# A two-layer attention kernel: ScalarE's copies ahead of exponentials in a layer's first steps, and another order of the work at the image's end

## The chip, the cores and the metric

The kernel runs on one core of one Trainium2 chip. The core has five engines that run side by side and meet by semaphores: TensorE (PE; its weight loads are shown as PEld), VectorE (DVE), ScalarE (ACT), GpSimd (POOL) and SyncE (SP), which starts the DMAs. The metric is the device time of one execution in microseconds; the figure of a version is the median of its runs.

## The reference

Two self-attention layers over eight images of 64x64 pixels and 64 channels, in float32:

```
xf = x.reshape(b, 4096, 64)
f, g, hh = xf @ wf + bf, xf @ wg + bg, xf @ wh + bh         # 8, 8 and 64 wide
x = gamma0 * softmax(g @ f.T) @ hh + x                      # layer 0

q, k, v = x @ Wq + bq, x @ Wk + bk, x @ Wv + bv             # 64 wide each
attn = softmax(q @ k.T)                                     # rows i, columns j
x = gamma1 * attn.T @ v + x                                 # layer 1
```

Layer 1 multiplies by the transposed attention matrix, so a row's sum must be known before the row's exponentials are used: the row of `v` is scaled by the row's weights (`v_scaled`), and the unscaled exponentials are the moving operand.

## The kernel before, in words

An image is 4096 positions, in 32 blocks of 128. The program handles two images in one pass of a hardware loop (four passes), each engine with its own instruction stream. An image has three parts.

**Layer 0** (`chunk0`): four chunks of 1024 queries, 32 steps each: two score matmuls (L499), ScalarE's exponential (L809), value matmuls (L515), and beside them matmuls and maxima of a coming chunk (L471, L977).

**Layer 1** (`steps1`): 32 rows of 128 queries, each cut into four pieces of 1024 keys. One piece is one step; 128 steps, eight (u0 to u7, two rows) to a pass of `t`. A step is:
- TensorE: `scores1` (L607), eight matmuls into two of four banks. It waits for VectorE's result of two steps before, since the banks alternate;
- VectorE: L1145 reads the scores, scales them into `e_whole` and takes the minimum (`bias_ready`);
- ScalarE: L872, the exponential in place with its sum (`exp1_done`), and after a row's fourth piece L878, the weights of its pieces (`chunk_w`);
- VectorE: `weigh_chunks` (L1121 to L1125) and `weigh_values` (L1134) make the row's `v_scaled`;
- TensorE: `values1` (L619), seven steps behind the scores (LAG1 = 7), into the four `sum_banks`.

In the first eight steps of layer 1 `sum_banks` aren't yet in use for values, and other work goes through them, two pairs called pair_c and pair_d. In the order in which TensorE has it (`between_scores`): a projection of q and k; after u1 the second half of `v` (L439); after u2 and u3 the transposes of the image after next (L419, `turn_x`), copied by VectorE (L952); after u4, u5 and u6 its projections pj0 to pj3 (L429; pj1 and pj2 both after u5). ScalarE copies out `v` (`projected_v`, L825) and the projections (`projected0`, L820). Each pair is written again after its copy only: `turn_x(2)` waits for the copy of `v` (`v1_sb`), pj2 for the copy of pj0, pj3 for that of pj1, and the first `values1` for that of pj2 (`pj_act`).

**The turn**, at the image's end: the last `values1` run; in between TensorE transposes eight units of the stacked f and g of the image after next (`turn_stack`, L463) into the `score_banks`, each copied by ScalarE (`turned_unit`, L842, `unit_sb`); VectorE scans x for its largest magnitude (`scan_x`, two parts, L958); from it TensorE computes a bound by one small matmul (`bound_of_qk`, L454), and VectorE derives powers of two and scales q's and k's weights by them (`scales`, L964 to L972, `w1s_ready`); VectorE adds the residual (L1191, `o_dve`, four parts); TensorE turns the result back (`turn_back`, L629, parts 2, 3, 0, 1), and VectorE and ScalarE copy it out (L1197, L895).

Each engine runs its list strictly as written; the order is written out by hand, and the semaphore waits in it are all there is of a schedule.

Of the kernel before, what the change touches and what calls it, by code (L numbers as in the profile page):

```python
# [21 lines left out]
AX_X = mybir.AxisListType.X  # L22
# [8 lines left out]
def attention_pair_kernel(nc, x, wf, bf, wg, bg, wh, bh, gamma0, wq, bq, wk, bk, wv, bv, gamma1, out):  # L31
# [44 lines left out]
    UNITS = 2 * NCH  # L76
    SCANS = 2
# [8 lines left out]
    with ExitStack() as ctx:  # L86
# [7 lines left out]
        score_banks = ctx.enter_context(nc.psum_tensor("score_banks", [P, 4, BANK], F32))  # L94
# [25 lines left out]
        x_abs2 = sb("x_abs2", [P, SCANS], F32)  # L120
        x_abs = sb("x_abs", [P, 1], F32)
# [292 lines left out]
        def _(pe):  # L414
# [269 lines left out]
            def image_steps(image, par):  # L684
                for q in range(NCH):
                    chunk0(image, par, q)
                ahead, last = image + 2, NCH - 1
                pe.wait_ge(a_used, ((image + 1) * NCH + 1) * TILES + EARLY * ATN + FREE_A)
                pe.wait_ge(w1s_ready, image + 1)
                pe.wait_ge(mid_ready, image * NCH + 3 + FREE)  # L690
                project_qk(par, 0, pair_c)
                values0(image, par, last, T - 4)

                def first_scores():
                    pe.wait_ge(low_done, 2 * (image * NCH + 2))
                    pe.wait_ge(k_copied[0], 32 * (image + 1))
                    scores1(image, 0, 0, 0)

                pe.wait_ge(exp0_done, (image + 1) * NCH * T - 1 + FREE_ST)
                project_qk(par, 1, pair_a)  # L700
                for i in range(T - 3, T):
                    values0(image, par, last, i)
                last_sums0(image, last)
                project_qk(par, 2, pair_b)
                pick0(image, last)
                first_scores()
                spread0(image, last)
                project_v(0, pair_c)

                def between_scores(u):  # L710
                    if u == 0:
                        pe.wait_ge(mid_ready, image * NCH + 4 + FREE)
                        project_qk(par, 3, pair_d)
                    elif u == 1:
                        pe.wait_ge(v1_sb, 2 * image + 1)
                        project_v(1, pair_c)
                    elif u == 2:
                        pe.wait_ge(x_loaded, 16 * (ahead + 1))
                        pe.wait_ge(low_done, 2 * (image * NCH + 4))
                        turn_x(0, pair_d[:, 0, :])  # L720
                        turn_x(1, pair_d[:, 1, :])
                    elif u == 3:
                        pe.wait_ge(v1_sb, 2 * image + 2)
                        turn_x(2, pair_c[:, 0, :])
                        turn_x(3, pair_c[:, 1, :])
                    elif u == 4:
                        pe.wait_ge(xt_dve, ahead * RT + 2)
                        project0(par, 0, pair_d)
                    elif u == 5:
                        pe.wait_ge(xt_dve, ahead * RT + 4)  # L730
                        project0(par, 1, pair_c)
                        pe.wait_ge(pj_act, ahead * RT + 1)
                        project0(par, 2, pair_d)
                    elif u == 6:
                        pe.wait_ge(pj_act, ahead * RT + 2)
                        project0(par, 3, pair_c)

                def steps1(t, first):
                    for u in range(U1):
                        if first and u == 1:  # L740
                            pe.wait_ge(low_done, 2 * (image * NCH + 3))
                        if first and 0 < u < NCH:
                            pe.wait_ge(k_copied[u], 32 * (image + 1))
                        if not first or u > 0:
                            scores1(image, t * 2 + u // NCH, t * U1 + u, u)
                        if first:
                            between_scores(u)
                        if first and u == LAG1:
                            pe.wait_ge(pj_act, ahead * RT + 3)
                        if t == 1 and u == 1:  # L750
                            pe.wait_ge(pj_act, ahead * RT + 4)
                        if not first or u >= LAG1:
                            values1(image, t, u - LAG1)

                for t in range(T // 2):
                    steps1(t, t == 0)
                for u in range(U1 - LAG1, NCH):
                    values1(image, T // 2 - 1, u)
                pe.wait_ge(f_stacked, (ahead + 1) * 4)
                pe.wait_ge(g_stacked, (ahead + 1) * 4)  # L760
                for n in range(4):
                    pe.wait_ge(bias_ready, (image + 1) * STEPS1 - (1 if n < 2 else 0) + FREE_S1)
                    turn_stack(n, score_banks[:, n, :])
                pe.wait_ge(unit_sb, ahead * UNITS + 1)
                bound_of_qk(ahead, score_banks[:, 0, :])
                for u in range(NCH, U1):
                    values1(image, T // 2 - 1, u)
                    if u == NCH + 1:
                        pe.wait_ge(w1s_ready, ahead + 1)
                        for n in range(4, 6):  # L770
                            pe.wait_ge(unit_sb, ahead * UNITS + n - 3)
                            turn_stack(n, score_banks[:, n - 4, :])
                for n in range(6, UNITS):
                    pe.wait_ge(unit_sb, ahead * UNITS + n - 3)
                    turn_stack(n, score_banks[:, n - 4, :])
                turn_back(image)

            with pe.Fori(0, B // 2) as two:
# [4 lines left out]
        def _(act):  # L783
# [68 lines left out]
            def image_steps(image, par):  # L852
# [15 lines left out]
                def steps1(t, first):  # L868
                    for u in range(U1):
                        step = image * STEPS1 + t * U1 + u  # L870
                        act.wait_ge(bias_ready, step + 1 + FREE_S1)
                        nc.scalar.activation(e_whole[:, u, :], e_whole[:, u, :], ACT.Exp, bias=exp_bias[:, u:u + 1],  # L872
                                             scale=-1.0, accum_out=part_sum[:, u // NCH, u % NCH:u % NCH + 1]
                                             ).then_inc(exp1_done, 1)
                        if u % NCH == NCH - 1:
                            odd = u // NCH
                            act.wait_ge(row_ready, image * T + t * 2 + odd + 1)
                            nc.scalar.activation(chunk_w[:, odd, :], exp_bias[:, odd * NCH:(odd + 1) * NCH], ACT.Exp,  # L878
                                                 scale=-1.0, bias=neg_row1[:, odd:odd + 1]).then_inc(chunk_w_ready, 1)
                        if first and u == 1:  # L880
                            projected_v(image, 1, pair_c)
                        if first and 4 <= u <= 7:
                            projected0(ahead, par, u - 4, pair_d if u % 2 == 0 else pair_c)

                steps1(0, True)
                with act.Fori(1, T // 2) as t:
# [16 lines left out]
        def _(dve):  # L903
# [47 lines left out]
                dve.wait_ge(xt_ps, image * RT + r + 1)  # L951
                nc.vector.tensor_copy(x_tr[par][:, r * BANK:(r + 1) * BANK], bank).then_inc(xt_dve, 1)  # L952

            def scan_x(image, par):
                dve.wait_ge(xt_dve, (image + 1) * RT)
                for j in range(SCANS):
                    cols = slice(j * (N // 2 // SCANS), (j + 1) * (N // 2 // SCANS))
                    chain.link(nc.vector.tensor_reduce(x_abs2[:, j:j + 1], x_tr[par][:, cols], AX_X, ALU.max,  # L958
                                                       apply_absolute_value=True))
                nc.vector.reduce_max(x_abs[:, :], x_abs2[:, :], AX_X).then_inc(x_abs_ready, 1)  # L960

            def scales(image, par, bank):
                dve.wait_ge(bound_ps, image + 1)
# [138 lines left out]
            def image_steps(image, par):  # L1102
# [78 lines left out]
                    steps1(t, False)  # L1181
                    assert chain.n == 2 * LINK_BLOCK
                rebase(start + PER_IMAGE - LINK_W - LINK_BOUND)
                scan_x(image + 2, par)
                weigh_chunks(T - 1, 1)
                weigh_values(T - 1, 1)
                scales(image + 2, par, score_banks[:, 0, :])

                for j in range(NCH):
                    dve.wait_ge(pv1_done, (image + 1) * STEPS1 - (NCH - 1 - j) + FREE_E1)  # L1190
                    nc.vector.scalar_tensor_tensor(out=o_tr[:, j, :], in0=sum_banks[:, j, :], scalar=gammas[:, 1:2],  # L1191
                                                   in1=mid_tr[:, j * BANK:(j + 1) * BANK], op0=ALU.mult, op1=ALU.add
                                                   ).then_inc(o_dve, 1)
# [33 lines left out]
```

## Time and profile before

| what | us |
|---|---|
| median of three runs | 4017.29 |
| lowest, highest | 4013.12, 4019.34 |
| profiled execution | 4017.23 |
| its span | 4015.2 |
| PE busy in the span | 3880.1 |
| DVE busy | 3186.7 |
| ACT busy | 2792.4 |
| POOL busy | 1944.6 |

The profile is one execution. A row of a timeline shows the start, the length, the engine, the line and what the instruction writes and reads; in brackets stands how long the engine had been idle before it, and which instruction ended that. Float32 matmuls appear as two instructions each. Matmuls overlap, so the step from start to start tells more than their lengths. The granted clock (PEclk) is 1.00 at TensorE's full level of 2.4 GHz and 0.50 at 1.2 GHz; over the whole span it is 0.979.

### The profile page before, as it was taken

The numbers are of one execution on the slowest core, as the hardware profiler recorded it, in microseconds if no ns is written. First come the engines' busy times: TensorE is split into PE (matmuls) and PEld (weight loads), VectorE is DVE, ScalarE is ACT, GpSimd is POOL, SyncE is SP. The second block draws the span as 40 slices with busy tenths as digits, with TensorE's granted clock in tenths as the row PEclk, the third lists the DMA queues.
The fourth block names the chain that finished last, engine by engine and source line by source line (L and its number), as shares of the span: only waits on it lengthen the run. The fifth ranks groups of instructions, "written<-read, shape, count | busy, mean of one in ns | idle before, by whom it ended". The sixth has DMA issues, their size and how long they took to land.

```text
span 4015.2 us, 81268 instructions
## 1 busy us (share of the span) xinstructions
PE 3880.1 (97%) x26001; PEld 1530.6 (38%) x26001; DVE 3186.7 (79%) x6206; ACT 2792.4 (70%) x3642; POOL 1944.6 (48%) x1031
## 2 busy tenths in 40 slices
PE   5999999999999999999999999999999999999999
PEld 3223552244422454225432255323443235522344
DVE  5677987778877888778877788777887779877788
ACT  1566777677767777767766677666776667767777
POOL 3696108941099312991139910498006961079410
PEclk7799999999999999999999999999999999999999
DMA  1000000000000000000000000000000000000000
GB/s 34 1 1 22 1 1 12 1 22 1 12 1 1 22 1 11 1 1 22 1 12 1 6 17 1 12 1 15 9 1 12 1 22 1 1 12 1 22 1 12
DMA packets 13910, 33.47 MB, mean 8 GB/s; under 512 B 3941, under 2 KB 3941, under 8 KB 12133
## 3 DMA queue, kind: packets, MB, share of 16 engines
q1 hardware_dynamic: 13540, 28.57, 2.5%
q8 instruction: 229, 3.75, 0.4%
q14 instruction: 141, 1.15, 0.1%
HBM read 11.78 MB, written 8.39 MB: 5 GB/s over the span
## 4 chain that ended last, share of the span: by engine, by line
PE 70%; issue 16%; POOL 6%; DVE 4%; ACT 3%; SPq 0%; POOLq 0%; DVEq 0%; DMA 0%; ACTq 0%
PE sum_banks L619 21%; PE score_banks L607 21%; PE sum_banks L515 14%; PE score_banks L499 7%; POOL e_sum L396 5%; PE sum_banks L537 3%; PE sum_banks L471 2%; DVE e_whole L1145 1%; ACT e_whole L809 1%; ACT g_tr L786 1%; DVE tile_max L977 1%; PE score_banks L463 1%; DVE x_abs L958 1%; PE sum_banks L556 1%; PE score_banks L482 0%
## 5 line engine op out<-in xcount | busy, mean ns | idle before, releaser
L977 DVE TENSOR_REDUCE tile_max<-sum_banks 128x1 f32<-128x512 f32 (+1 forms) x2128 | 1367.5, 686 | 513.7 <-PE sum_banks L471 508.8
L396 POOL TENSOR_TENSOR e_sum<-e_sum,e_whole 128x1024 f32<-128x1024 f32 x704 | 1660.9, 2359 | 104.2 <-ACT e_whole L809 56.9
L809 ACT ACTIVATE e_whole<-score_banks,no_bias,down 128x1024 f32<-128x1024 f32 x1024 | 1229.4, 1205 | 522.4 <-PE score_banks L499 470.7
L872 ACT ACTIVATE e_whole<-e_whole,exp_bias 128x1024 f32<-128x1024 f32 x1024 | 1177.8, 1150 | 475.7 <-DVE e_whole L1145 459.0
L1145 DVE TENSOR_SCALAR_CACHE_REDUCE e_whole<-score_banks,neg_down 128x1024 f32<-128x1024 f32 x1024 | 1293.3, 1282 | 122.3 <-PE score_banks L607 111.7
L515 PE MATMUL sum_banks<-e_whole,proj 128*64 128x512 f32 x4096 | 1122.2, 627 | 0.0
L619 PE MATMUL sum_banks<-e_whole,v_scaled 128*64 128x512 f32 x4096 | 1063.9, 593 | 13.6 <-ACT proj L820 11.1
L607 PE MATMUL score_banks<-k_high,q_split 128*64 128x512 f16 x4096 | 824.8, 380 | 2.3 <-DVE e_whole L1145 1.8
L607 PE MATMUL score_banks<-k_low,q_split 128*64 128x512 f16 x4096 | 823.1, 379 | 0.0
L471 PE MATMUL sum_banks<-f_tr,g_tr 33*128 33x512 f16 x2128 | 689.5, 400 | 14.7 <-DVE tile_max L977 10.1
L499 PE MATMUL score_banks<-g_tr,f_tr 34*128 34x512 f16 x2048 | 636.0, 390 | 17.4 <-ACT g_tr L786 8.8
L607 PEld LDWEIGHTS score_banks<-k_high,q_split 128*64 128x64 f16 x4096 | 267.3, 109 | 399.0 <-DVE e_whole L1145 158.8
L607 PEld LDWEIGHTS score_banks<-k_low,q_split 128*64 128x64 f16 x4096 | 272.1, 110 | 331.5 <-issue 239.1
L619 PEld LDWEIGHTS sum_banks<-e_whole,v_scaled 128*64 128x64 f32 x4096 | 326.6, 137 | 171.7 <-issue 37.0
L499 PEld LDWEIGHTS score_banks<-g_tr,f_tr 34*128 34x128 f16 x2048 | 118.9, 94 | 715.2 <-issue 595.1
L393 POOL TENSOR_TENSOR e_sum<-e_whole 128x1024 f32<-128x1024 f32 x32 | 75.3, 2353 | 564.0 <-ACT e_whole L809 564.0
L515 PEld LDWEIGHTS sum_banks<-e_whole,proj 128*64 128x64 f32 x4096 | 207.9, 136 | 312.0 <-ACT e_whole L809 159.6
L355 POOL TENSOR_TENSOR proj<-proj,b 128x256 f32<-128x256 f32 (+1 forms) x66 | 56.2, 852 | 391.1 <-DVE e_whole L1145 391.1
L471 PEld LDWEIGHTS sum_banks<-f_tr,g_tr 33*128 33x128 f16 x2128 | 176.1, 94 | 151.6 <-DVE tile_max L977 68.4
L872 ACT ACTIVATION_READ_ACCUMULATOR e_whole<-e_whole,exp_bias 128x1 f32 x1024 | 191.8, 187 | 0.0
L537 PE MATMUL sum_banks<-e_whole,ones_w 128*32 128x256 f32 x2048 | 164.5, 393 | 0.0
L1134 DVE TENSOR_TENSOR v_scaled<-v,norm_w 128x256 f32<-128x256 f32 x256 | 108.9, 425 | 62.4 <-DVE norm_w L1125 60.2
(132 smaller groups left out, 1654.0 us busy)
## 6 DMA issues: line engine op xcount, KB each, us to landing
x_in<-in_x_dram SPq DMA_DIRECT2D x11, 1024.0 KB, 4.9
out_dram<-y_out SPq DMA_DIRECT2D x32, 256.0 KB, 2.8
k_high<-k_high SPq DMA_DIRECT2D x32, 128.0 KB, 2.2
k_low<-k_low SPq DMA_DIRECT2D x32, 128.0 KB, 2.2
w<-in_L_conv_wg_dram SPq DMA_DIRECT2D x2, 2.0 KB
w<-in_L_conv_wf_dram SPq DMA_DIRECT2D x2, 2.0 KB
w<-in_L_conv_wh_dram SPq DMA_DIRECT2D x2, 16.0 KB
b<-in_L_conv_bh_dram SPq DMA_DIRECT2D x1, 32.0 KB
```

Source lines behind the costliest of these rows:

```text
L396: nc.gpsimd.tensor_tensor(acc, acc, e_whole[:, i % U0, :], ALU.add).then_inc(e_added, 1)
L471: nc.tensor.matmul(sum_banks[:, (2 + j % banks) % 4, :], g_tr[HIGH:KX, par, q * CH + blk * P:q * CH + (blk + 1) * P], f_tr[HIGH:KX, par, j ...
L499: mm = nc.tensor.matmul(score_banks[:, 2 * (i % 2) + h, :], f_tr[0:KM, par, i * P:(i + 1) * P], g_tr[0:KM, par, q * CH + h * BANK:q * CH + ...
L515: mm = nc.tensor.matmul(sum_banks[half * C:(half + 1) * C, 0, :], proj[:, par, i, GFW:PW], e_whole[:, i % U0, half * BANK:(half + 1) * BAN ...
L537: mm = nc.tensor.matmul(sum_banks[rows, 1, 0:SQ], ones_w[:, :], terms[:, c * SQ:(c + 1) * SQ], start=first, stop=final, skip_group_check=True)
L607: mm = nc.tensor.matmul(bank[c * C:(c + 1) * C, :], q_split[:, query_col(i) + c * C:query_col(i) + (c + 1) * C], k_part[:, col:col + BANK] ...
L619: mm = nc.tensor.matmul(sum_banks[half * C:(half + 1) * C, j, :], v_scaled[:, u // NCH, j, :], half_of_chunk(u, half), start=i == 0, stop= ...
L809: nc.scalar.activation(e_whole[:, i % U0, :].rearrange("p (a n) -> p a n", a=2), score_banks[:, 2 * (i % 2):2 * (i % 2) + 2, :], ACT.Exp, ...
L872: nc.scalar.activation(e_whole[:, u, :], e_whole[:, u, :], ACT.Exp, bias=exp_bias[:, u:u + 1], scale=-1.0, accum_out=part_sum[:, u // NCH, ...
L977: nc.vector.reduce_max(tile_max[:, blk, j:j + 1], sum_banks[:, (2 + j % banks) % 4, :], AX_X).then_inc(a_used, 1)
L1134: nc.vector.tensor_tensor(v_scaled[:, par, :, :], v1[:, i, :].unsqueeze(1).to_broadcast([P, NCH, C]), norm_w[:, par, :].unsqueeze(2).to_br ...
L1145: nc.vector.tensor_scalar(e_whole[:, u, :], score_banks[:, 2 * (u % 2):2 * (u % 2) + 2, :] .rearrange("p a n -> p (a n)"), neg_down[:, par ...
```

## The change

Two things are moved; nothing is computed otherwise.

In the first eight steps of layer 1, ScalarE's copy of the second half of `v` stands before the exponential of u1 (it stood behind it). The copies of pj0 and pj1 stand before the exponentials of u4 and u5, and those of pj2 and pj3 behind the exponentials of u5 and u6, where they stood behind those of u6 and u7.

In the turn, VectorE does one part of the scan, then the last row's `weigh_chunks` and `weigh_values`, then the other part. TensorE's bound matmul goes from before `values1` of u4 to behind `turn_stack(5)` (bank 3 in place of bank 0, so after unit 3's copy); the scales on VectorE stand behind two of the four residual additions; TensorE's wait for `w1s` stands before `turn_stack(7)`, whose bank the bound was in.

```
@@ TensorE, turn @@
-                pe.wait_ge(unit_sb, ahead * UNITS + 1)
-                bound_of_qk(ahead, score_banks[:, 0, :])
                 for u in range(NCH, U1):
                     values1(image, T // 2 - 1, u)
                     if u == NCH + 1:
-                        pe.wait_ge(w1s_ready, ahead + 1)
                         for n in range(4, 6):
                             pe.wait_ge(unit_sb, ahead * UNITS + n - 3)
                             turn_stack(n, score_banks[:, n - 4, :])
-                for n in range(6, UNITS):
-                    pe.wait_ge(unit_sb, ahead * UNITS + n - 3)
-                    turn_stack(n, score_banks[:, n - 4, :])
+                        pe.wait_ge(unit_sb, ahead * UNITS + 4)
+                        bound_of_qk(ahead, score_banks[:, 3, :])
+                turn_stack(6, score_banks[:, 2, :])
+                pe.wait_ge(w1s_ready, ahead + 1)
+                turn_stack(7, score_banks[:, 3, :])
                 turn_back(image)
@@ ScalarE, steps of layer 1 @@
                     for u in range(U1):
                         step = image * STEPS1 + t * U1 + u
+                        if first and u == 1:
+                            projected_v(image, 1, pair_c)
+                        if first and 4 <= u <= 5:
+                            projected0(ahead, par, u - 4, pair_d if u % 2 == 0 else pair_c)
                         act.wait_ge(bias_ready, step + 1 + FREE_S1)
                         nc.scalar.activation(e_whole[:, u, :], e_whole[:, u, :], ACT.Exp, bias=exp_bias[:, u:u + 1],
...
-                        if first and u == 1:
-                            projected_v(image, 1, pair_c)
-                        if first and 4 <= u <= 7:
-                            projected0(ahead, par, u - 4, pair_d if u % 2 == 0 else pair_c)
+                        if first and 5 <= u <= 6:
+                            projected0(ahead, par, u - 3, pair_c if u % 2 == 0 else pair_d)
@@ VectorE @@
-            def scan_x(image, par):
+            def scan_x(image, par, parts=range(SCANS)):
                 dve.wait_ge(xt_dve, (image + 1) * RT)
-                for j in range(SCANS):
+                for j in parts:
...
-                nc.vector.reduce_max(x_abs[:, :], x_abs2[:, :], AX_X).then_inc(x_abs_ready, 1)
+                if SCANS - 1 in parts:
+                    nc.vector.reduce_max(x_abs[:, :], x_abs2[:, :], AX_X).then_inc(x_abs_ready, 1)
...
-                scan_x(image + 2, par)
+                scan_x(image + 2, par, range(1))
                 weigh_chunks(T - 1, 1)
                 weigh_values(T - 1, 1)
-                scales(image + 2, par, score_banks[:, 0, :])
-
+                scan_x(image + 2, par, range(1, SCANS))
                 for j in range(NCH):
+                    if j == 2:
+                        scales(image + 2, par, score_banks[:, 3, :])
                     dve.wait_ge(pv1_done, (image + 1) * STEPS1 - (NCH - 1 - j) + FREE_E1)
```

ScalarE in the first steps, before, from the exponential of u4 (L872 is an exponential, L820 a copy of a projection, L878 the row's weights):

```order
L872 ACTIVATE e_whole,part_sum<-e_whole,exp_bias 128x1024 [waits bias_ready]
L819 ISA
L820 COPY proj<-sum_banks 128x2x4x80 [waits pj_ps]
L871 REGISTER_ALU
L872 ACTIVATE e_whole,part_sum<-e_whole,exp_bias 128x1024 [waits bias_ready]
L819 REGISTER_ALU
L820 COPY proj<-sum_banks 128x2x4x80 [waits pj_ps]
```

The same place in the changed kernel, from u3's row weights (the exponential is now L875, the copy L819, the weights L881):

```order
L881 ACTIVATE chunk_w<-exp_bias,neg_row 128x4 [waits row_ready]
L818 ISA
L819 COPY proj<-sum_banks 128x2x4x80 [waits pj_ps]
L874 REGISTER_ALU
L875 ACTIVATE e_whole,part_sum<-e_whole,exp_bias 128x1024 [waits bias_ready]
L818 REGISTER_ALU
L819 COPY proj<-sum_banks 128x2x4x80 [waits pj_ps]
```

Each exponential and the copy behind it have changed places, so pj0 follows the row's weights at once; u1's exponential and the copy of `v` have changed places in the same way.

TensorE in the turn, before, from the end of unit 3 (L463 turns a unit, L454 is the bound, L619 values):

```order
L454 MATMUL score_banks<-x_coef,x_abs 128x1 [waits x_abs_ready,unit_sb]
L616 REGISTER_ALU
L619 MATMUL sum_banks<-e_whole,v_scaled 64x512 [waits exp1_done,v_scaled_ready]
L619 MATMUL sum_banks<-e_whole,v_scaled 64x512
L619 MATMUL sum_banks<-e_whole,v_scaled 64x512 [waits exp1_done]
L619 MATMUL sum_banks<-e_whole,v_scaled 64x512
L463 MATMUL score_banks<-ident_h,f_stack 128x128 [waits unit_sb,w1s_ready]
```

The changed kernel, from the second value group of the turn on:

```order
L463 MATMUL score_banks<-ident_h,g_stack 128x128 x7
L770 REGISTER_ALU
L454 MATMUL score_banks<-x_coef,x_abs 128x1 [waits x_abs_ready,unit_sb]
L619 MATMUL sum_banks<-e_whole,v_scaled 64x512 [waits exp1_done]
L619 MATMUL sum_banks<-e_whole,v_scaled 64x512
L619 MATMUL sum_banks<-e_whole,v_scaled 64x512 [waits exp1_done]
L619 MATMUL sum_banks<-e_whole,v_scaled 64x512
L463 MATMUL score_banks<-ident_h,f_stack 128x128 x8
L463 MATMUL score_banks<-ident_h,g_stack 128x128 [waits w1s_ready]
```

The bound has gone behind units 4 and 5, and the wait for `w1s` from unit 4 to unit 7.

VectorE in the turn, before (L958 a part of the scan, L1121 to L1134 the last row's weights and `v_scaled`, L964 the first of the scales):

```order
L958 TENSOR_REDUCE x_abs<-x_tr 128x1
L918 REGISTER_ALU
L958 TENSOR_REDUCE x_abs<-x_tr 128x1
L918 REGISTER_ALU
L960 TENSOR_REDUCE x_abs<-x_abs 128x1
L1119 REGISTER_ALU
L1120 REGISTER_ALU
L1121 ISA part_scr,row_sum<-part_sum,chunk_w 128x4
```

And in the changed kernel, from `v_scaled` on (L1136), with the scan now L959, the residual additions L1194 and the scales from L966:

```order
L1136 TENSOR_TENSOR v_scaled<-v,norm_w 128x256
L959 TENSOR_REDUCE x_abs<-x_tr 128x1
L919 REGISTER_ALU
L962 TENSOR_REDUCE x_abs<-x_abs 128x1
L1193 ISA
L1194 SCALAR_TENSOR_TENSOR o_tr<-sum_banks,gammas,mid_tr 128x512
L1193 REGISTER_ALU
L1194 SCALAR_TENSOR_TENSOR o_tr<-sum_banks,gammas,mid_tr 128x512
L966 TENSOR_TENSOR bound<-score_banks,b_coef 128x1
```

The second part of the scan now stands behind `v_scaled`, and the scales behind two additions.

## Rows read from the trace of the kernel before

**Rows 1.** TensorE's waits from 300 us on: waited for, total us, times, longest.
```profile
PE sum_banks L619 <- ACT proj L820: 11.1, 8, 1.4
PE sum_banks L419 <- ACT v L825: 8.9, 8, 1.1
...
PE sum_banks L429 <- ACT proj L820: 5.9, 8, 0.7
PE sum_banks L619 <- DVE v_scaled L1134: 2.5, 8, 0.3
```

**Rows 2.** Timeline of TensorE, image 7's first steps: start, length, instruction, idle before.
```profile
3777.89 1.09 PE L419 MATMUL sum_banks<-ident,x_in 128*128 128x128 f32 x8 [1.12 <-ACT v L825]
3778.92 0.41 PE L607 MATMUL score_banks<-k_high,q_split 128*64 128x512 f16 x2
...
3779.90 1.12 PE L429 MATMUL sum_banks<-w,x_tr 64*128 64x80 f32 x16
3780.95 0.41 PE L607 MATMUL score_banks<-k_high,q_split 128*64 128x512 f16 x2
...
3783.80 1.12 PE L429 MATMUL sum_banks<-w,x_tr 64*128 64x80 f32 x16 [0.74 <-ACT proj L820]
...
3789.33 1.08 PE L619 MATMUL sum_banks<-e_whole,v_scaled 128*64 128x512 f32 x4 [1.39 <-ACT proj L820]
```

**Rows 3.** Timeline of ScalarE, same stretch.
```profile
3775.70 1.15 ACT L872 ACTIVATE e_whole<-e_whole,exp_bias 128x1024 f32<-128x1024 f32 x1 [1.77 <-DVE e_whole L1145]
...
3776.85 0.99 ACT L825 COPY v<-sum_banks 128x1024 f32<-128x1024 f32 x1
...
3780.46 0.28 ACT L878 ACTIVATE chunk_w<-exp_bias,neg_row 128x4 f32<-128x4 f32 x1
3781.93 1.15 ACT L872 ACTIVATE e_whole<-e_whole,exp_bias 128x1024 f32<-128x1024 f32 x1 [1.19 <-DVE e_whole L1145]
...
3783.08 0.67 ACT L820 COPY proj<-sum_banks 128x640 f32<-128x640 f32 x1
3783.65 1.15 ACT L872 ACTIVATE e_whole<-e_whole,exp_bias 128x1024 f32<-128x1024 f32 x1
```

**Rows 4.** Timeline of VectorE, same stretch.
```profile
3779.40 1.29 DVE L952 COPY x_tr<-sum_banks 128x512 f32<-128x512 f32 x2
3780.61 1.27 DVE L1145 TENSOR_SCALAR_CACHE_REDUCE e_whole<-score_banks,neg_down 128x1024 f32<-128x1024 f32 x1
```

**Rows 5.** Timeline of all engines, the last turn.
```profile
3997.99 2.47 DVE L958 TENSOR_REDUCE x_abs<-x_tr 128x1 f32<-128x1024 f32 x2
...
3998.95 0.28 ACT L878 ACTIVATE chunk_w<-exp_bias,neg_row 128x4 f32<-128x4 f32 x1
...
4001.40 0.34 PE L454 MATMUL score_banks<-x_coef,x_abs 128*128 128x1 f32 x2
4001.57 0.43 DVE L1134 TENSOR_TENSOR v_scaled<-v,norm_w 128x256 f32<-128x256 f32 x1 [0.21 <-DVE norm_w L1125]
4001.91 0.15 DVE L964 TENSOR_TENSOR bound<-score_banks,b_coef 128x1 f32<-128x1 f32 x1
...
4002.05 1.94 PE L619 MATMUL sum_banks<-e_whole,v_scaled 128*64 128x512 f32 x8 [0.31 <-DVE v_scaled L1134]
...
4002.81 0.28 DVE L972 TENSOR_SCALAR w1s<-w,up 128x128 f32<-128x128 f32 x1
...
4002.98 1.04 ACT L842 COPY g_tr<-score_banks 128x1024 f16<-128x1024 f16 x1
...
4006.04 1.61 DVE L1191 SCALAR_TENSOR_TENSOR o_tr<-sum_banks,gammas,mid_tr 128x512 f32<-128x512 f32 x2 [1.26 <-PE sum_banks L619]
...
4007.69 1.92 PE L629 MATMUL sum_banks<-ident,o_tr 128*128 128x128 f32 x16
```

**Rows 6.** Busy time by stretch, 30 us from a turn: least and most of seven.
```profile
1573.00:1603.00 30.00, 28.29 (x168) 9.51 (x169) 21.43 (x39) 21.70 (x22) 17.11 (x8) 0.89 0.10 36
2056.00:2086.00 30.00, 25.83 (x134) 8.28 (x136) 17.14 (x33) 17.79 (x19) 11.91 (x6) 0.77 0.12 39
```

## The prediction

> **What bounds the kernel now.** I read the list of TensorE's waits first. For the second layer it names four waits that come eight times each, once per image: value matmuls for ScalarE's `proj` copies (11.1 us), turns of `x_in` for its copy of `v` (8.9), projections for its `proj` copies (5.9), value matmuls for VectorE's `v_scaled` (2.5) [rows 1]. Eight times the longest is about the total in each, so every image has the same. Next to them the list has little for this layer, where TensorE works back to back: a wait removed there is time removed, if nothing else is late in its place. Then TensorE's timeline of the first steps of image 7, with idle time in brackets: 1.12 before the turns of x, 0.74 before the third projection, 1.39 before the first value matmuls [rows 2]; beside it ScalarE [rows 3] and VectorE [rows 4], and last the turn at the image's end [rows 5].
>
> I call the first eight steps u0 to u7, and the four projections of x and their copies pj0 to pj3.
>
> **The first steps.** Nothing is added: the copy of `v` goes before the exponential of u1, and each of four `proj` copies goes ahead of one exponential. Why they were late is in ScalarE's rows. It works in order. It idled 1.77 us until VectorE had the scores of u1, did that exponential (1.15) and only then the copy of `v` [rows 3], though TensorE had done the matmuls of `v` before the scores of u2. In the same way it idled 1.19 us before the exponential of u4 (3781.93) and copied pj0 only at 3783.08 [rows 3], while pj0's matmuls had started at 3779.90 and were over by 3780.95, when the next scores began [rows 2].
>
> Now the chain, with distances from start to start: turns of x to scores 1.03, scores to projection 0.98, projection to scores 1.05 [rows 2]; I use 1.05 between two projections and 0.98 from scores to values too.
> - The copy of `v` (0.99) fits whole in the 1.77 us before u1's exponential, which stays at 3775.70. TensorE then turns x at 3777.89 - 1.12 = 3776.77; scores u4 3777.80, pj0 3778.78, scores u5 3779.83, pj1 3780.81.
> - pj1 needs VectorE's copies of x, 3779.40 to 3780.69 [rows 4], which VectorE cannot do earlier: 0.12 to spare. pj2 follows at 3781.86 and needs pj0's copy. ScalarE is through with u3's `chunk_w` at 3780.46 + 0.28 = 3780.74, the copy takes 0.67: 3781.41. No wait.
> - Scores u6, 3782.91, need VectorE's u4, done 3780.61 + 1.27 = 3781.88 [rows 4]: no wait. pj3, 3783.89, needs pj1's copy. The exponential of u4 stays at 3781.93, so that copy runs 3783.08 to 3783.75: 0.14 to spare.
> - Scores u7 3784.94, value matmuls 3785.92. They need pj2's copy: exponential u5 at 3783.65 [rows 3], copy at 3784.80, done 3785.47. 0.4 to spare, less what a weight load needs.
> So the first values start at 3785.92 instead of 3789.33: 3.41 us. The idle times alone give 1.12 + 0.74 + 1.39 = 3.25; they are counted from modelled ends, so I take the distances, 3.41.
>
> What is late next: the exponentials of u4 to u7 come behind a copy each. From 3785.47 on, u6, pj3's copy and u7 end by 3788.4 (1.15 + 0.67 + 1.15). u7's values are wanted seven steps after the first ones, each longer than the 0.98 of its scores, so after 3792.7. VectorE wants the last `chunk_w` (3788.7) after the next u1, whose scores end no sooner than 3785.92 + 2 x 0.98 and take VectorE 1.27: 3789.2. The short path, scores waiting for VectorE two steps back, has no ScalarE in it. If one of these covers failed, TensorE would wait that much, at most a copy's 0.67 per image.
>
> **The turn.** Before, VectorE did both parts of the scan (2.47 from 3997.99, to 4000.46), then the row's weights and `v_scaled`, ready at 4002.00, 1.54 later; TensorE's values started at 4002.05 after 0.31 idle [rows 5]. Now one part (1.23) is done at 3999.22, as is ScalarE's `chunk_w` (3998.95 + 0.28), so `v_scaled` is ready by 3999.23 + 1.54 = 4000.8. TensorE, without the bound's matmul, gets to the values at 4001.40: no wait, 0.6 to spare. The bound's matmul (0.34) is moved, not saved: it stands behind two units, near 4004.1, and needs the copy of unit 3, which ended at 4004.02 [rows 5]. Just in time, up to 0.1 lost.
>
> The scales: from the bound to VectorE's first instruction 0.51 (4001.40 to 4001.91), through `w1s` 1.18 (to 4003.09) [rows 5], so `w1s` at 4005.8 to 4005.9. TensorE wants it before the last unit. The third residual addition started at 4006.04, 3.99 after the values of u4 [rows 5]; by TensorE it could now start at 4001.40 + 3.99 + 0.34 = 4005.73, but the scales hold it to about 4006.0, where it is now. Behind those values TensorE has another value group (half of 1.94) and a unit, so it comes to the last one near 4006.9: 1 us to spare. The turn back starts 0.31 sooner than its 4007.69, at 4007.38, and needs the third addition (4006.85) and, a quarter (0.48) later, the fourth (4007.65) [rows 5]: 0.2 to spare. So the turn gives the 0.31 that TensorE stood still; bounds 0 and 0.4.
>
> **Sum.** 3.41 + 0.31 = 3.72 us per image, times eight: 29.8 us. The profiled execution took 4017.23 (span 4015.2), 0.06 from the median 4017.29. 4017.2 - 29.8 = 3987.4 us.
>
> **What the clock adds.** After each turn but the last the granted clock falls for a while: over 30 us it reads 0.89 in two of seven, 0.77 in two, 0.83 in three between [rows 6]. That is (1 - 0.89) x 2 x 30 = 6.6 us at the half level of 1.2 GHz, or 13.8, or 10.2; in all 71.4 us. A microsecond there costs at most half of one. All seven short would make 46 us, all long 97: up to 12.8 us less or more in time. The change leaves the idle spell before them as it is but moves each by 3.7 us more than the last. By the rows alone nothing shifts, and the sum stays 3987.4.
>
> The Trainium skill (TensorE: Matmul & The Clock Gate, "What's actually happening") says that idleness brings the slow level back, and that the gate counts freely, not from the program's start. By that rule the seven lengths are drawn anew, anywhere in 3987.4 +- 12.8. The trace agrees, in that like turns got 6.6 and 13.8 us.
>
> I put no shift into the sum and some 5 us either way into the range, since seven draws seldom all fall to one side.
>
> **Rivals.**
> - The spare times of 0.1 to 0.2 us are used up and shorter waits return: at the x copies, at pj1's and pj2's copy about 0.3 us each, and the turn's gain is lost: 8 x (3.41 - 0.9) = 20 us, 3997. For it: those are the tightest numbers above. Against: the waits follow each other, so that a link late once makes the next less so.
> - The change doesn't do what it says: the `proj` copies were late because of their projections, not of the exponentials. Only the wait for `v` and the turn would count: 8 x (1.12 + 0.31) = 11.4, 4005.8. Against: pj0's matmuls were over two microseconds before its copy [rows 2, 3].
> - Slower: in the turn VectorE's scales now stand behind two additions, and the bound behind a ScalarE copy. If `w1s` came later than 4006.9, TensorE would stand before the last unit, and the clock could fall inside the turn, whose 7.5 us of matmuls (4002.05 to 4007.69 + 1.92) would take double: 8 x 7.5 = 60 us more, less 29.8: 4047. Against: every input of the scales has its row, and it has 1 us to spare.
>
> **Chances.** Forecast 0.82, spare times used up 0.11, copies held by TensorE 0.05, slower 0.02. The likeliest case's own range is 3982 to 3994; with the first rival and the clock's ends, 3979 to 4001. About 0.2%, or 8 us, is what can be told from no change. The second rival, at 11.4 us, falls inside that with a bad draw of the clock. Faster 0.94, same 0.04, slower 0.02.
>
> **What would show it.** Right: the waits for `v` and for `proj` copies gone from TensorE's list; from the turns of x to the first values 9.15 us (3776.77 to 3785.92), where it was 11.44 (3777.89 to 3789.33); no idle before the turn's values. Wrong: a new wait of scores for VectorE, idle before the bound's matmul or the turn back, or a clock column below 0.77 after the turns.

## The result, and the profile after

| | before | changed |
|---|---|---|
| median, four runs each | 4018.32 us | 3978.19 us |
| lowest, highest | 4013.12, 4021.24 | 3977.26, 3979.42 |
| profiled execution, its span | 4017.23, 4015.2 | 3977.29, 3975.3 |

The medians differ by 40.1 us, where 29.8 were forecast. The ratio, estimated from all the runs, is 0.9906 (95% interval 0.9895 to 0.9918). As a time, 3978.19 lies 0.8 us below the lower end of the prediction's range, 3979, and 4 below that of the likeliest case, 3982; as a ratio it is just inside (3979 divided by the prediction's 4017.3 is 0.9905), since the kernel before has a median 1 us higher here. It is more than the mechanism gives; much of this section and of the experiments is about the 10 us between.

First TensorE's waits of the changed kernel from 300 us on, as in [rows 1] (waited for, total us, times, longest):

```profile
PE score_banks L482 <- POOL c_stack L320: 26.2, 29, 1.3
PE score_banks L499 <- issue: 9.0, 3, 3.0
PE score_banks L499 <- ACT g_tr L785: 6.8, 29, 0.2
PE sum_banks L471 <- DVE tile_max L979: 5.7, 20, 0.5
PE score_banks L607 <- DVE e_whole L1147: 1.9, 8, 0.2
```

All four waits of [rows 1] are gone, and none of the list's length has come in their place in layer 1; the last row, 0.23 us per image, was there before (1.8 in all).

TensorE's timeline of the first steps of image 7, as in [rows 2]:

```profile
3738.50 1.09 PE L419 MATMUL sum_banks<-ident,x_in 128*128 128x128 f32 x8
3739.82 0.41 PE L607 MATMUL score_banks<-k_high,q_split 128*64 128x512 f16 x2 [0.23 <-DVE e_whole L1147]
...
3740.81 1.10 PE L419 MATMUL sum_banks<-ident,x_in 128*128 128x128 f32 x8
3741.83 0.41 PE L607 MATMUL score_banks<-k_high,q_split 128*64 128x512 f16 x2
...
3744.85 2.02 PE L429 MATMUL sum_banks<-w,x_tr 64*128 64x80 f32 x32
...
3747.90 1.12 PE L429 MATMUL sum_banks<-w,x_tr 64*128 64x80 f32 x16
...
3749.84 1.04 PE L619 MATMUL sum_banks<-e_whole,v_scaled 128*64 128x512 f32 x4
```

From the second turns of x to the first values it is 3749.84 - 3740.81 = 9.03 us; 9.15 was forecast, 11.44 it was. From the first turns of x (3738.50) it is 11.34. Before, these stood here, and the first values at 3789.33, 14.93 later:

```profile
3774.40 1.09 PE L419 MATMUL sum_banks<-ident,x_in 128*128 128x128 f32 x8
```

I use this last distance below, since the experiments differ ahead of the second turns. pj1 and pj2 now are one run of 32 matmuls. Behind the second turns one place isn't back to back: pj3 starts 1.10 us after its scores (3746.80 to 3747.90), where the other projections start 0.98 or 0.99 after theirs. That is a wait of 0.12 us, too short for the list; what ended it is read from ScalarE below.

ScalarE beside it, as in [rows 3]:

```profile
3737.93 0.99 ACT L824 COPY v<-sum_banks 128x1024 f32<-128x1024 f32 x1
3739.80 1.15 ACT L875 ACTIVATE e_whole<-e_whole,exp_bias 128x1024 f32<-128x1024 f32 x1 [0.88 <-DVE e_whole L1147]
...
3744.74 0.67 ACT L819 COPY proj<-sum_banks 128x640 f32<-128x640 f32 x1
3746.03 1.15 ACT L875 ACTIVATE e_whole<-e_whole,exp_bias 128x1024 f32<-128x1024 f32 x1 [0.61 <-DVE e_whole L1147]
...
3747.18 0.67 ACT L819 COPY proj<-sum_banks 128x640 f32<-128x640 f32 x1
```

The copies lie in idle time that ScalarE had: 1.77 before u1's exponential has become 0.88, 1.19 before u4's has become 0.61. Both exponentials still wait for VectorE, not for the copy. pj1's copy ends at 3747.18 + 0.67 = 3747.85, right before pj3: here TensorE does wait for a copy.

The turn of the last image, all engines, as in [rows 5]:

```profile
3958.46 1.22 DVE L959 TENSOR_REDUCE x_abs<-x_tr 128x1 f32<-128x1024 f32 x1
...
3960.08 0.62 PE L463 MATMUL score_banks<-ident_h,f_stack 128*128 128x128 f16 x8
...
3960.78 0.43 DVE L1136 TENSOR_TENSOR v_scaled<-v,norm_w 128x256 f32<-128x256 f32 x1 [0.21 <-DVE norm_w L1127]
...
3961.43 0.61 PE L463 MATMUL score_banks<-ident_h,g_stack 128*128 128x128 f16 x8
...
3961.97 1.94 PE L619 MATMUL sum_banks<-e_whole,v_scaled 128*64 128x512 f32 x8
...
3964.30 0.61 PE L463 MATMUL score_banks<-ident_h,g_stack 128*128 128x128 f16 x8
...
3964.74 0.33 PE L454 MATMUL score_banks<-x_coef,x_abs 128*128 128x1 f32 x2
3965.01 1.94 PE L619 MATMUL sum_banks<-e_whole,v_scaled 128*64 128x512 f32 x8
...
3966.03 0.28 DVE L974 TENSOR_SCALAR w1s<-w,up 128x128 f32<-128x128 f32 x1
3966.23 1.52 DVE L1194 SCALAR_TENSOR_TENSOR o_tr<-sum_banks,gammas,mid_tr 128x512 f32<-128x512 f32 x2
...
3967.33 0.61 PE L463 MATMUL score_banks<-ident_h,g_stack 128*128 128x128 f16 x8
...
3967.78 1.92 PE L629 MATMUL sum_banks<-ident,o_tr 128*128 128x128 f32 x16
```

`v_scaled` is ready at 3961.21 and wanted at 3961.97: 0.76 to spare. `w1s` is ready at 3966.31, the last unit starts at 3967.33. From the first unit to the turn back it is 7.70 us. Before, the units stood here, and the turn back at 4007.69:

```profile
3999.61 0.62 PE L463 MATMUL score_banks<-ident_h,f_stack 128*128 128x128 f16 x8
...
4000.96 0.61 PE L463 MATMUL score_banks<-ident_h,g_stack 128*128 128x128 f16 x8
...
4004.37 0.61 PE L463 MATMUL score_banks<-ident_h,g_stack 128*128 128x128 f16 x8
...
4004.91 1.94 PE L619 MATMUL sum_banks<-e_whole,v_scaled 128*64 128x512 f32 x8
```

That is 8.08, so 0.38 gained, where 0.31 was forecast. It is a difference of two: from unit 3 to the values went 1.09 (4000.96 to 4002.05) and now go 0.54, and from unit 5 to the next values went 0.54 and now, with the bound's matmul between, 0.71. So 0.55 less 0.17.

So an image gained (14.93 - 11.34) + 0.38 = 3.97 us, eight times: 31.8. All eight images have these distances to 0.01. The profiled executions differ by 39.9. The other 8 us lie outside the changed stretches. The first turns of x, image 0, before and then changed:

```profile
376.65 1.09 PE L419 MATMUL sum_banks<-ident,x_in 128*128 128x128 f32 x8
```

```profile
371.28 1.09 PE L419 MATMUL sum_banks<-ident,x_in 128*128 128x128 f32 x8
```

5.4 us are there already. Of all that was moved only the copy of v has run by then, half a microsecond before. The busy time by stretch (span of the stretch, then PE, PEld, DVE, ACT, POOL busy, and PEclk, the granted clock) names the place, before and changed:

```profile
126.00:136.00 10.00, 9.74 (x27) 1.80 (x27) 7.03 (x11) 6.74 (x6) 7.36 (x4) 0.50 0.00 0
136.00:146.00 10.00, 10.00 (x42) 1.70 (x40) 4.58 (x8) 4.12 (x4) 4.97 (x3) 0.61 0.00 0
```

```profile
126.00:136.00 10.00, 9.79 (x34) 1.92 (x34) 7.05 (x12) 6.44 (x6) 8.68 (x4) 0.61 0.00 0
136.00:146.00 10.00, 10.00 (x64) 2.42 (x61) 7.28 (x13) 6.69 (x7) 8.82 (x5) 1.00 0.02 3
```

TensorE's clock rose from 1.2 to 2.4 GHz about 10 us sooner in this execution, in the first chunk of image 0, with TensorE busy 9.7 and 10.0 of 10 us, and long before the first moved instruction: 10 us at half speed is 5 us. Of the remaining 2.7 us, 2.5 lie between the turns and the next x turns, seven times, where the clock falls.

### The profile page after: what moved, and what is told of

Its sections match the earlier page's. It is cut to its first block, busy times and chain, and to the rows that moved or that the text cites. A ratio compares the mean times of both kernels' runs of the same rounds, so it can differ in the third digit from the quotient of the medians.

```text
span 3975.3 us, 81252 instructions
## 1 busy us (share of the span) xinstructions
PE 3869.3 (97%) x26001; PEld 1476.7 (37%) x26001; DVE 3185.5 (80%) x6206; ACT 2790.6 (70%) x3642; POOL 1943.7 (49%) x1031
## 4 chain that ended last, share of the span: by engine, by line
PE 72%; issue 16%; POOL 6%; DVE 3%; ACT 3%; SPq 0%; POOLq 0%; DVEq 0%; DMA 0%; ACTq 0%
PE sum_banks L619 22%; PE score_banks L607 21%; PE sum_banks L515 13%; PE score_banks L499 7%; POOL e_sum L396 6%; PE sum_banks L537 2%; PE sum_banks L471 2%; ACT e_whole L808 1%; PE score_banks L463 1%; ACT g_tr L785 1%; DVE tile_max L979 1%; DVE e_whole L1147 1%; PE sum_banks L556 1%; PE score_banks L482 0%; PE score_banks L447 0%
## 5 line engine op out<-in xcount | busy, mean ns | idle before, releaser
L875 ACT ACTIVATE e_whole<-e_whole,exp_bias 128x1024 f32<-128x1024 f32 x1024 | 1175.9, 1148 | 447.9 <-DVE e_whole L1147 430.4
L619 PE MATMUL sum_banks<-e_whole,v_scaled 128*64 128x512 f32 x4096 | 1054.6, 593 | 0.0
L607 PE MATMUL score_banks<-k_high,q_split 128*64 128x512 f16 x4096 | 806.9, 380 | 2.3 <-DVE e_whole L1147 1.9
L607 PE MATMUL score_banks<-k_low,q_split 128*64 128x512 f16 x4096 | 805.2, 379 | 0.0
L499 PE MATMUL score_banks<-g_tr,f_tr 34*128 34x512 f16 x2048 | 634.9, 389 | 18.3 <-issue 9.0
L607 PEld LDWEIGHTS score_banks<-k_high,q_split 128*64 128x64 f16 x4096 | 251.2, 109 | 415.5 <-DVE e_whole L1147 160.5
L607 PEld LDWEIGHTS score_banks<-k_low,q_split 128*64 128x64 f16 x4096 | 254.3, 110 | 349.2 <-issue 246.9
L619 PEld LDWEIGHTS sum_banks<-e_whole,v_scaled 128*64 128x64 f32 x4096 | 308.4, 137 | 174.2 <-issue 24.6
L875 ACT ACTIVATION_READ_ACCUMULATOR e_whole<-e_whole,exp_bias 128x1 f32 x1024 | 191.0, 187 | 0.0
L1136 DVE TENSOR_TENSOR v_scaled<-v,norm_w 128x256 f32<-128x256 f32 x256 | 109.0, 426 | 62.4 <-DVE norm_w L1127 60.2
```

Source lines behind the costliest of these rows:

```text
L499: mm = nc.tensor.matmul(score_banks[:, 2 * (i % 2) + h, :], f_tr[0:KM, par, i * P:(i + 1) * P], g_tr[0:KM, par, q * CH + h * BANK:q * CH + ...
L607: mm = nc.tensor.matmul(bank[c * C:(c + 1) * C, :], q_split[:, query_col(i) + c * C:query_col(i) + (c + 1) * C], k_part[:, col:col + BANK] ...
L619: mm = nc.tensor.matmul(sum_banks[half * C:(half + 1) * C, j, :], v_scaled[:, u // NCH, j, :], half_of_chunk(u, half), start=i == 0, stop= ...
L1136: nc.vector.tensor_tensor(v_scaled[:, par, :, :], v1[:, i, :].unsqueeze(1).to_broadcast([P, NCH, C]), norm_w[:, par, :].unsqueeze(2).to_br ...
```

## The experiments

Times are medians, and differences in us are of medians; the ratios are estimated from all the runs. "Before" is the kernel before, run on the same chip beside each of three groups of experiments, where it had 4013.8 us (18 runs, for the parts of the change), 4012.03 (19 runs, for the changed kernel again and the added matmuls) and 4014.68 (7 runs, for the row maxima), with single runs from 4005.9 to 4021.2. Distance A is from the first turns of x to the first values (14.93 before, 11.34 changed); distance B is from the turn's first unit to the turn back (8.08 and 7.70). Both come from TensorE's timeline, and hold in all eight images unless said otherwise.

### The parts of the change

**ScalarE's order alone** (e1_acts): the ScalarE part of the change's diff, nothing of TensorE and VectorE.

> ScalarE's new order alone, the turn as before. Theory: the three waits go in full without the turn's help. From the turns of x (first transpose) to the first value matmuls 11.34 us instead of 14.93, as in the whole change; first unit's turn to turn back stays 8.08. 8 x 3.59 = 28.7 us faster, give or take what the stretches at the slow clock do (some 5 us). Rival: part of the 3.59 comes from the turn's order, then the distance stays above 11.6.

3984.23 us, ratio 0.9930 (0.9911 to 0.9949): 29.6 faster. A is 11.34, B is 8.08. The three waits go without any help of the turn, as the theory had it.

**The turn alone** (e2_turn): the other two parts of the diff.

> The new turn alone, ScalarE's order as before. Theory: first unit's turn to turn back 7.70 instead of 8.08 us, turns of x to first values stays 14.93: 8 x 0.38 = 3.0 us faster. Rival (the 8 us of the whole change that my sum did not have come from the turn, by way of the clock after it): 8 to 11 us faster, and the first scores after the turn back to the next x turns shorter in every image.

4010.10 us, ratio 0.9989 (0.9980 to 0.9999): 3.7 faster. B is 7.70, A is 14.93 (15.02 in one image). The distances between the turn back and the next x turns are no shorter than before: 1766.7 us in all seven, 1765.1 before. So the rival, 8 to 11 us by way of the clock, isn't borne out.

**The copy of v alone** (e3_vcopy):

```
+                        if first and u == 1:
+                            projected_v(image, 1, pair_c)
                         act.wait_ge(bias_ready, step + 1 + FREE_S1)
...
-                        if first and u == 1:
-                            projected_v(image, 1, pair_c)
```

> Only the copy of v goes before the exponential of u1. Theory (waits in series): the 1.12 us before the turns of x goes, but pj0's copy still starts behind the exponential of u4, which VectorE sets, so pj2 starts when it did and its wait grows from 0.74 to about 1.9: from VectorE's u4 on nothing is earlier, 0 us gained (within 0.1 per image). Rival (waits add up): 1.12 to 1.2 us per image, 9 to 10 us faster.

4025.20 us, ratio 1.0031 (1.0020 to 1.0041): 11.4 us slower than before. A is 14.93 in five images, so moving this copy alone gains nothing, as the theory had it: the wait has only moved. In three images it is longer, up to 16.26, which no theory had. TensorE in image 7, and the busy time of that stretch and of one in image 4 (PEclk is the third figure from the end):

```profile
3779.02 1.12 PE L429 MATMUL sum_banks<-w,x_tr 64*128 64x80 f32 x16
3782.07 1.59 PE L429 MATMUL sum_banks<-w,x_tr 64*128 64x80 f32 x16 [1.93 <-ACT proj L820]
3783.59 0.64 PE L607 MATMUL score_banks<-k_high,q_split 128*64 128x512 f16 x2
```

```profile
3781.00:3787.00 6.00, 4.93 (x44) 3.31 (x46) 2.56 (x9) 2.86 (x7) 0.00 (x0) 0.72 0.01 3
2325.00:2336.00 11.00, 9.40 (x64) 5.12 (x66) 4.78 (x13) 7.09 (x13) 0.00 (x0) 0.69 0.01 5
```

The 1.12 us before the second turns of x went, and pj2's wait grew from 0.74 to 1.93. Behind the one long wait the granted clock fell (0.72 and 0.69 over these stretches), and a pair of score matmuls took 0.64 instead of 0.41. From the first turns of x to the turn's first unit it is 226.7 to 226.8 us in these three images, where it was 225.1 to 225.2 before: 4.8 us in all. In the kernel before, where the same idle time comes in pieces of 1.12 and 0.74, the trace shows no such fall in these steps, in eight images. The profiled execution is the fastest of this kernel's nine (4016.97), and it had the early first turns of x (371.28). So the trace accounts for 4.8 of the 11.4 us; what the clock did in the other executions no trace shows.

**The proj copies alone** (e4_proj): the change's diff for `projected0`, with the copy of v left behind the exponential.

> Only the proj copies go ahead, the copy of v stays behind the exponential of u1. Theory: the wait for v stays at 1.12, those of pj2 and of the values go: first values 2.3 us earlier per image (distance from the turns of x 12.6), 18 to 19 us faster. Together with the previous kernel's 0 this is less than the whole 3.59: the copy of v is worth 1.2 us only with the others. Rival (additive): 0.74 + 1.39 = 2.13, 17 us.

3995.48 us, ratio 0.9954 (0.9935 to 0.9972): 18.3 faster. A is 12.41: 2.52 per image, 20 us in all, more than the 2.3 of the theory and the 2.13 of the rival. So, by A, the parts are worth 0 and 2.52 alone and 3.59 together. The copy of v is worth 1.07 once the others have gone ahead: waits in series, not added. Here pj3 starts 0.99 after its scores, without the 0.12 of the whole change, since TensorE comes there later beside ScalarE.

### The 8 us that the mechanism doesn't give

**The changed kernel again** (e5_after_again): no edit.

> The changed kernel once more, on one chip with the following ones, for the 8 us by which its first profile was faster than my sum. Theory: they were drawn, not made: 5.4 us of them lay ahead of the first changed instruction (first x turns at 371.28 instead of 376.65 us) and the rest in stretches between a turn's end and the next x turns. Then the distances repeat (x turns to values 11.34, turn 7.70), the first x turns move by several us between profiles, and the gain against before is 32 us plus or minus 5. Rival: the change brings the clock's part with it; then the first x turns are at 371.3 again and the gain is 40.

3978.88 us (3978.01 to 3980.29), ratio 0.9920 (0.9904 to 0.9937) against 19 runs of before: 33.1 us faster, not 40. A and B are the same. The two expectations mixed their marks: the first turns of x were at 371.87, near the first profile's 371.28, as the rival said, while the gain was the theory's 33. The other profiles help. All these kernels have the same list on TensorE as before up to these turns. The one with only the copy of v moved had them at 371.28 too, and the kernel with all of ScalarE's order here:

```profile
375.44 1.09 PE L419 MATMUL sum_banks<-ident,x_in 128*128 128x128 f32 x8
```

The turn alone had 375.43, the `proj` copies alone 374.11, and before 376.65. The granted clock from 136 to 146 us goes with it: 1.00 in the three early ones, 0.61, 0.67, 0.69 and 0.81 in before and the other three. So an early start doesn't follow what was moved. That it is drawn anew at each execution isn't shown by this: the only kernel with two profiles had 371.28 and 371.87. Of the first comparison's 40 us, 4 to 6 are that before's four runs there had a median that much higher than its many runs later (4018.3 against 4012.0 to 4014.7). 33.1 against 31.8 is the better comparison. Why the changed kernel's runs lie within 3 us in both comparisons, and before's within 8 and 13, stays open.

**More matmuls where TensorE has little to do.** The clock falls after each turn but the last, and costs some us each time. I tried to hold it up with matmuls of 512 columns and 34 rows whose result nobody reads. The edit on the changed kernel, in two blocks: f1_fill3 has the first block alone, f2_fill3_tail both, f3_fill5_tail both with five in place of three.

```
+                    if q == 0 and i < LAG0:
+                        if i == 0:
+                            pe.wait_ge(y_act, image * (NCH // 2) + FREE_Y)
+                        filler(par, sum_banks[:, 0, :], 3)
...
                 turn_back(image)
+                if par == 1:
+                    pe.wait_ge(unit_sb, ahead * UNITS + 5)
+                    filler(par, score_banks[:, 0, :], 8)
```

> The changed kernel with three more 512-column matmuls (results never read) in each of the first four steps of an image, where TensorE has little to do; 96 in all. Theory: the granted clock falls after a turn because TensorE stands idle or thinly used for the first steps. With the extra work it stays at 1.00 after the turns of images 0, 2, 4 and 6, which have no idle spell before the scores: about 3 us saved at each, 10 to 14 us in all; after the others it may still fall. Rival: the clock falls anyway, the extra work is paid for: 0 to 5 us slower.

> The same, and eight more such matmuls behind the turn back of every second image, where TensorE otherwise stands 2.9 us at the loop's branch. Theory: now the clock holds after the odd turns too, 20 to 28 us faster than the changed kernel. Rival: the matmuls don't overlap the branch's delay, and 1.7 us is added to each of three turns: no more than the kernel with three alone, or 5 us less.

> Five extra matmuls per step instead of three, with the same eight behind every second turn back. If three are too thin to hold the clock, five hold it (25 us faster than the changed kernel); if three hold it, five only cost: up to 0.4 us in each of 32 steps where they pass what the step has free, some 5 us slower than with three.

3984.15, 3998.51 and 4018.84 us, where the changed kernel had 3978.88 on the same chip: 5, 20 and 40 us slower. The theory failed in all three; three alone came out as its rival had it, 0 to 5 us slower. Busy time over 30 us behind image 1's turn, of the changed kernel, of three and of three with the tail:

```profile
1080.00:1110.00 30.00, 26.28 (x134) 7.24 (x132) 19.34 (x30) 19.33 (x18) 19.48 (x9) 0.83 0.12 39
```

```profile
1085.00:1115.00 30.00, 27.13 (x124) 7.32 (x124) 17.50 (x29) 16.78 (x16) 18.93 (x9) 0.77 0.11 38
```

```profile
1090.00:1120.00 30.00, 28.51 (x122) 7.34 (x122) 15.73 (x25) 15.02 (x15) 17.05 (x8) 0.72 0.11 38
```

Here TensorE is busier (26.28, 27.13, 28.51 of 30 us), and the clock lower, not higher (0.83, 0.77, 0.72); ScalarE's busy time goes from 19.33 to 15.02. But this is one turn of seven. The granted clock over 30 us from each of the seven turns back, on average:

| kernel | seven turns | after images 0, 2, 4, 6 |
|---|---|---|
| changed | 0.84 | 0.89, 0.83, 0.83, 0.83 |
| changed, again | 0.83 | 0.83, 0.83, 0.89, 0.89 |
| three | 0.85 | 0.89, 0.89, 0.94, 0.89 |
| three, tail | 0.80 | 0.83, 0.77, 0.77, 0.94 |
| five, tail | 0.79 | 0.83, 0.89, 0.83, 0.89 |

So the clock fell in every kernel after every turn. Three alone left its average where it was, and the 5 us are the price of the extra work; with the tail the average is lower. Behind the turns of images 0, 2, 4 and 6 the first two kernels with added matmuls run the same code, and differ there by up to 0.17, so a good part of such a difference is the execution's and not the code's. The tail itself cost little: TensorE's idle time at the loop's branch went from 9.0 us in three times to 3.9, and the first scores came 5.03 to 5.07 us behind the turn back instead of 4.85 to 4.93. So the rival of f2_fill3_tail, that these matmuls would not fit into the idle time and add 1.7 us each time, didn't come true either. These matmuls use 34 of 128 rows; whether wider ones would hold the clock wasn't tried.

### The next wait on the list

**Row maxima a step later** (g1_mrow27; two steps: g2_mrow28). The longest wait left was for GpSimd, in layer 0. The edit of g1_mrow27 on the changed kernel (g2_mrow28 has `LAST + 4`):

```
-    MROW_AT = LAST + 2
+    MROW_AT = LAST + 3
```

> The changed kernel, with layer 0's matmuls for the next chunk's row maxima (L482) one step later, at step 27 instead of 26 of 32. After the change TensorE's longest wait in total is there: 26.2 us in 29 waits for GpSimd's c_stack, at most 1.3, since GpSimd has a queue of 2.36 us additions ahead of it. A step is 1.55 us long. Theory (a wait on one engine that comes 1.3 us or less too late goes when the work stands a step later, as in the change): all waits gone, 26 us faster than the changed kernel, some 58 faster than before. Rival: it turns into another wait, for ScalarE's copy of the rows or GpSimd's e_sum, and less than 10 us are gained.

> The same two steps later, at step 28. If one step was enough, nothing more comes of it, and the copy (1.00 us) comes nearer to the next chunk's first scores, which need it: same as step 27, or up to 0.5 us per chunk slower. If the waits at step 27 are still half there, this takes the rest.

One step later: 3938.95 us (3936.63 to 3939.95), ratio 0.9808 (0.9792 to 0.9825) against before, 39.9 us less than the changed kernel's 3978.88, which was taken on another chip, and the best version here. Its waits from 300 us on:

```profile
PE score_banks L499 <- issue: 8.3, 3, 3.0
PE sum_banks L471 <- DVE tile_max L979: 5.0, 17, 0.5
PE score_banks L607 <- DVE e_whole L1147: 1.8, 8, 0.2
```

The wait for GpSimd (26.2) and the one behind it for ScalarE's copy (6.8) are both gone, and 3.4 us of the same two ahead of 300 us: 36.4 of the 39.3 us between the two profiled executions. The expectation, 26, had left out the wait for the copy; its rival had that copy as the wait that would come instead. Two steps later: 3947.02 us (3938.34 to 3948.18), ratio 0.9823 (0.9806 to 0.9841), and the second one is back:

```profile
PE score_banks L499 <- ACT g_tr L785: 6.8, 29, 0.2
```

The rest of step 28's 8 us isn't accounted for; the two intervals overlap.

## Why the prediction was right

- **What bounds the kernel.** Right. Removing TensorE's waits of layer 1 removed that time; nothing came in its place but 0.12 us per image at pj3.
- **First steps, 3.41 per image.** Right in mechanism, 0.18 too small: 3.59, shown alone by ScalarE's order (A 11.34 there too). Between the first and the second turns of x 1.18 went (3.49 to 2.31), where the sum took the idle time of 1.12. Behind the second turns the sum was 0.12 too long: pj1 and pj2 together take 1.95 (3744.85 to the next scores at 3746.80), not 1.05 and 1.05, and from the last scores to the values it is 0.89 (3748.95 to 3749.84), not 0.98; pj3's wait of 0.12 goes against that. The spare time of 0.12 at the x copies was enough. That of 0.14 at pj1's copy was not, since TensorE came there 0.15 earlier than in the sum: this is the small wait of the first rival, in one place.
- **The turn, 0.31.** Right in kind; 0.38, shown alone by B. The sum took the idle time of 0.31 ahead of the values and up to 0.1 for the bound; by the distances it is 0.55 and 0.17.
- **The exponentials behind the copies.** Right: no wait for any of them. The second rival gave the copy of `v` a worth of its own (8 x (1.12 + 0.31)). In this chain it has none: alone it gains nothing, and that kernel was 11 us slower, of which the trace gives 4.8 to the clock.
- **The sum.** 29.8 forecast; the distances give 31.8, and the comparison with 19 runs of before 33.1. The rest of the first 40.1 isn't the mechanism's: 5.4 us between the two profiles lie ahead of the first turns of x, and before's median was 4 to 6 us lower later. These parts carried the result to the range's lower end; that it went no further was luck and no merit of the sum.
- **The clock.** The term that was mis-sized. I gave it 5 us either way, counted from the seven falls after the turns only. These gave 1.8: by the granted clock over 30 us the changed kernel has 0.89 once and 0.83 six times, 67.8 us at the half level, where before had 71.4. The rise in the first chunk, which moved by 10 us between executions of kernels with the same TensorE list up to there, was left out, and so was the spread of before's own runs, 4005.9 to 4021.2, which alone makes 15. What the prediction took from the Trainium skill (TensorE: Matmul & The Clock Gate, "What's actually happening"), that the gate counts freely, agrees with this in so far as programs that are the same up to there came to the first turns of x 5.4 us apart. Why the rise moved by 10 us no run here shows.

## What to carry to other kernels

Read the waits of the engine that is always busy; if an engine that works in order holds it up, look what stands ahead of the awaited instruction there and whether that itself waits for something else. Waits of one chain don't add up: simulate the chain, start to start, since moving one link alone can gain nothing, and gathering idle time in one piece can cost the clock. And where a first comparison gives more than the distances between marks in the two traces, look for the difference ahead of the part that was changed.

## What the runs showed of the hardware

- One idle spell of 1.93 us on TensorE was followed by the half clock (1.2 GHz) in three of eight images, at a cost of some 1.5 us each; spells of 1.12, 0.74 and 1.39 us, each followed by work, by none in eight.
- Extra matmuls of 34 rows did not keep the clock up: on average over 30 us behind the turns 0.85, 0.80 and 0.79, where the changed kernel had 0.84 and 0.83. In image 1 TensorE was busy 27.1 and 28.5 of 30 us instead of 26.3, and the clock 0.77 and 0.72 instead of 0.83.
- Eight matmuls put ahead of the hardware loop's branch fitted into the idle time there: 9.0 us in three times became 3.9, and the next scores came 0.1 to 0.2 us later.
- TensorE's clock rose in the first chunk about 10 us apart in two executions whose programs don't differ up to there.
